# A gated cross-attention block with a routed feed-forward: keys staged first in each GpSimd slot, router weights cast in slot 2, and the first router step in two parts

## The chip, the cores and the metric

The kernel runs on one core of a Trainium2 chip. The metric is device time in microseconds (us), from the runtime's measurement of one execution. A core has five engines that run beside each other, each through its own queue in strict order: TensorE (PE) does matmuls and transposes into PSUM, VectorE (DVE) and ScalarE (ACT) read and write PSUM and SBUF, GpSimd (POOL) works on SBUF only, and SyncE (SP) issues DMAs. They meet at semaphores: an instruction that waits holds all that is queued behind it on its engine.

## What is computed

x is 16 batches of 128 tokens of 128 features; the context is 16 batches of 77 rows of 96.

```python
def xattn(x, y):                       # 16 heads of 8 features
    q = x @ Wq.T + bq;  k, v = split(y @ Wkv.T + bkv)
    att = softmax(q k / sqrt(8), over the 77 rows)
    return (att v) @ Wo.T + bo

def ffn(x):                            # 4 rounds, 4 experts, 2 of them per token
    cur = x
    for r in range(4):
        logits = cur @ Wg[r] + bg[r]
        vals, idx = top_k(logits, 2);  w = softmax(vals)
        cw = sum(one_hot(idx, 4) * w)
        y = gelu(cur @ W1[e] + b1[e]) @ W2[e] + b2[e]      # for each expert e
        cur = cur + sum_e(cw[e] * y[e])
    return cur

x = x + tanh(g0) * xattn(layernorm(x), ctx)
x = x + tanh(g1) * ffn(layernorm(x))
```

## The kernel before

All tensors stay on chip. There are two parts. The first is attention, in 16 **slots**, b = 0 to 15, one batch each, software-pipelined over the engines. The second is the experts: 16 steps (4 rounds of 4 chunks of 512 tokens) of 4 experts, 64 units, each unit an `up` and a `down` of TensorE, in three matmuls for each product (high by high, low by high, high by low parts), with gelu and the high parts on ScalarE and the low parts on VectorE.

What an engine does in a slot is written by hand, in the order of the code of its block, and tables (`K_AT`, `XN_AT`, `MOMENTS`, `SPLIT_X` and others) say which slot holds an extra step. In slot b:

- TensorE computes `scores(b + 1)` (line 1261), transposes the exponents' inputs of batch b in three groups (line 1275), projects the output of batch b - 2 (`project_o`, line 1310), and weighs the values of batch b - 1, called PV(b - 1) (lines 1297 and 1303). `scores(b)` waits for `k_st` of batch b, which is the keys spread over head-masked rows, and for the subtracted scores of batch b - 1. It does not wait for the exponentials. Slots 2, 5 and 8 hold transposes of the normalised x (line 1225), slots 10 and 13 transposes of the second normalisation's x (line 1321), slots 13 and 15 the logits of routers 0 and 1 (lines 1336 and 1337), slot 15 the transpose of router 0's weights (line 1383). Then `up(0)` starts, and PV(15) follows it.
- VectorE normalises the output of batch b - 2 (`normalise_o`: a reciprocal, line 918, writes `rT_sb`; line 922 writes `oT_sb`), takes the least score of batch b + 1 (line 902, in two halves), adds the residual of batch b - 3 (line 928) and subtracts (line 911). Behind these come the extra steps: moments of a layer norm (lines 862 and 865), the split of a chunk into high and low parts (`split_x`, lines 943 and 945), the router, the weights.
- ScalarE subtracts the other half of the scores (line 717), takes the exponentials in three groups (line 727) and moves some results out of PSUM. `gate` (line 743) is the tanh of a router step, `move_cwT` (line 762) moves the transposed weights. After the last slot come gate(1), a table load and the gelus.
- GpSimd stages the keys (`stage_k`, line 597, two batches ahead of the slot), ends the layer norms (`rstd_of`, lines 567 and 569; four normalisations at a time, lines 576 and 586), adds a bias to x (line 606), makes the low parts of the expert weights (`split_w`, lines 615 and 617) and the small tables of the router (`expert_order`, lines 554 to 560).
- SyncE loads inputs, places the values' pieces, and spreads the routed weights over the partitions.

**The first router step** is spread over slots 12 to 15. In slot 12 VectorE makes three copies of the router weights `wg_in` (line 1144 a cast into `wg_s`, line 1146 the rest of it, line 1149 `wg_w`). In slot 13 `router(0)` adds two logits parts and a bias (lines 1000 and 1002) and ranks the four experts (lines 1010 to 1028, nine small operations that end in `half_d`). ScalarE takes the tanh in slot 14, VectorE makes the weights in slot 14 (`weights(0)`, lines 1042 and 1050) and splits chunk 1. Slot 15 holds the moments of chunk 2 and `router(1)` with all its eleven operations. `stage_k` stands behind the other work of a slot from slot 2 on:

```python
                if b < 2:
                    stage_k(b + 2)
...
                if b - W_LAG in W_AT:
                    split_w(W_AT.index(b - W_LAG))
                if 2 <= b < B - 2:
                    stage_k(b + 2)
```

Of the kernel before, what the change touches and what calls it, by code (L numbers as in the profile page):

```python
# [15 lines left out]
def flamingo_gated_block(  # L16
# [59 lines left out]
    with ExitStack() as stack:  # L76
# [105 lines left out]
        gates_ld = sem("gates_ld")  # L182
        moe_ld = sem("moe_ld")
        out_st = sem("out_st")
        c_zero = sem("c_zero")
# [100 lines left out]
        CWT0_AT = 15  # L286
        GATE0_SLOT = 14
        ROUTER0_SLOT = 13
        WEIGHTS0_SLOT = 14
        ROUTER1_SLOT = 15  # L290
        K_AT = {8: 3}
# [113 lines left out]
        MOMENTS = {3: (0, 2), 5: (0, 3), 8: (1, 0), 10: (1, 1), 15: (1, 2)}  # L405
        SPLIT_X = {10: 0, 14: 1}

# [3 lines left out]
        def LG(q):  # L411
            return bank(("LG", q))[:, 0:TC * 2 * E]
# [31 lines left out]
        def _(sp):  # L444
# [15 lines left out]
            sp.dma_start(bg_row[:, :], bg.rearrange("r e -> (r e)").unsqueeze(0)  # L460
                          .to_broadcast([P, ROUNDS * E])).then_inc(moe_ld, 16)
            sp.dma_start(wg_in[:, :, :], Wg.rearrange("r h e -> h r e")).then_inc(moe_ld, 16)
            def place_v(c):
# [52 lines left out]
        def _(pool):  # L516
# [92 lines left out]
            def split_w(p):  # L609

                s = slice(p * WP, (p + 1) * WP)
                if p == 0:
                    pool.wait_ge(w_hi, 32)
                    pool.wait_ge(moe_ld, 16 * 4)
                nc.gpsimd.tensor_tensor(w1_lo[:, s], w1_in[:, s], w1_hi[:, s].bitcast(F32),
                                        ALU.subtract).then_inc(w_split, 1)
                nc.gpsimd.tensor_tensor(w2_lo[:, s], w2_in[:, s], w2_hi[:, s].bitcast(F32),
                                        ALU.subtract).then_inc(w_split, 1)
# [13 lines left out]
            for b in range(B):  # L632
                if b < 2:
                    stage_k(b + 2)
# [14 lines left out]
                if b - W_LAG in W_AT:  # L649
                    split_w(W_AT.index(b - W_LAG))  # L650
                if 2 <= b < B - 2:
                    stage_k(b + 2)
                if b % TC == 0:
# [14 lines left out]
        def _(act):  # L668
# [112 lines left out]
            for b in range(B):  # L781
                c, r = b // TC + 1, b % TC
                exponentials(b, 2)
                if b == GATE0_SLOT:
                    gate(0)
                if b not in BUSY and b + 1 < B:
                    subtract_most(b + 1)
                exponentials(b, 1)
                if b in XT_AT:
                    move_cur(XT_AT.index(b))  # L790
                if b == CWT0_AT:
                    move_cwT(0)
                if b in XN_AT:
                    move_xn(XN_AT[b])
                if b in BUSY and b + 1 < B:
                    subtract_most(b + 1)
                if b in Q_AT:
                    stage_q(Q_AT[b])
                exponentials(b, 0)
                if b in V_AT:  # L800
                    move_v(V_AT[b])
                if b in K_AT:
                    move_k(K_AT[b])
# [49 lines left out]
        def _(dve):  # L853
# [121 lines left out]

            def router(q):

                if q == 0:
                    dve.wait_ge(order_ready, 2)
                t = [gate_ops(q)]  # L980

# [10 lines left out]
                bgr = bg_row[:, r * E:(r + 1) * E].unsqueeze(1).to_broadcast([P, T, E])  # L992
                if q < 2:
                    written(dve, ("LG", q))
                    dve.wait_ge(moe_ld, 16 * 4)
                else:
                    dve.wait_ge(logits_done, q - 1)
                if q < 2:
                    lg_v = LG(q).rearrange("p (t n) -> p t n", t=T)
                    step(nc.vector.tensor_tensor(lga[:, ts, :], lg_v[:, :, 0:E], bgr, ALU.add))  # L1000
                    settle()
                    step(nc.vector.tensor_tensor(lg[:, ts, :], lg_v[:, :, E:2 * E], lga[:, ts, :], ALU.add))
                else:
                    lg_v = ps[:, 6 if q < NC else 7, 0:T * 32].rearrange("p (t w) -> p t w", t=T)
                    step(nc.vector.tensor_tensor(lg[:, ts, :], lg_v[:, :, 0:E], bgr, ALU.add))
                settle()
# [104 lines left out]
            for b in range(B):  # L1111
# [9 lines left out]
                if b + 1 < B:  # L1121
                    subtract(b + 1)
                if b == WEIGHTS0_SLOT:
                    weights(0)
                if b in MOMENTS:
                    moments(*MOMENTS[b])
                if b in NORMALISE:
                    normalise(NORMALISE[b])
                if b == 0:
# [5 lines left out]
                    copy_k(2)  # L1135
                if b == ROUTER0_SLOT:
                    router(0)
                if b in SPLIT_X:
                    split_x(SPLIT_X[b])
                if b == ROUTER1_SLOT:  # L1140
                    router(1)
                if b == 12:
                    dve.wait_ge(moe_ld, 16 * 4)
                    nc.vector.tensor_copy(wg_s[:, :, 0, :], wg_in[:, :, :]).then_inc(wg_split, 1)
# [419 lines left out]
```

## Time and profile before

| what | value |
|---|---|
| runs of the kernel before | 466.62 us median of 3 (466.54 to 467.97) |
| the profiled execution | 466.59 us |
| its span, first to last instruction | 464.9 us |
| granted TensorE clock, of full speed | 0.999 |
| TensorE busy | 451.3 us, 97% |
| VectorE busy | 366.3 us, 79% |
| ScalarE busy | 360.0 us, 77% |
| GpSimd busy | 70.0 us, 15% |

Attention fills the span to about 91 us, the experts the rest. The profile follows the work that ended last back from the end; 85% of the span on that chain is TensorE, 7% VectorE, 3% issue, 2% ScalarE. The rows of the next sections are from the trace of that execution. A row of a timeline has the start in us, the duration in us, the engine, the line of the kernel, the operation, what is written and read, the shapes and the count of merged instructions; a bracket at the end is the time for which the engine had been idle before, and what released it. "PE" is TensorE's matmul side.

### The profile page before, as it was taken

The numbers are of one execution on the slowest core, as the hardware profiler recorded it, in microseconds if no ns is written. First come the engines' busy times: TensorE is split into PE (matmuls) and PEld (weight loads), VectorE is DVE, ScalarE is ACT, GpSimd is POOL, SyncE is SP. The second block draws the span as 40 slices with busy tenths as digits, with TensorE's granted clock in tenths as the row PEclk, the third lists the DMA queues.
The fourth block names the chain that finished last, engine by engine and source line by source line (L and its number), as shares of the span: only waits on it lengthen the run. The fifth ranks groups of instructions, "written<-read, shape, count | busy, mean of one in ns | idle before, by whom it ended". The sixth has DMA issues, their size and how long they took to land.

```text
span 464.9 us, 8783 instructions
## 1 busy us (share of the span) xinstructions
PE 451.3 (97%) x2856; PEld 354.8 (76%) x2856; DVE 366.3 (79%) x729; ACT 360.0 (77%) x742; POOL 70.0 (15%) x109
## 2 busy tenths in 40 slices
PE   8988998899999999999999999999999999999996
PEld 6665766677877788878878887888788878888885
DVE  6987989988888779767876887688768876887776
ACT  5766877497878779877987798779877887787883
POOL 7928966125000000000000000000000000000000
PEclk9999999999999999999999999999999999999999
DMA  6690000050020200400030013002200310023001
GB/s 164 199 191 15 1 6 14 1 183 2 1 91 2 91 2 2 182 1 1 25 159 1 1 49 135 0 1 80 104 0 0 119 66 1 0 69 138 24 0 45
DMA packets 12892, 25.18 MB, mean 54 GB/s; under 512 B 4615, under 2 KB 8496, under 8 KB 10800
## 3 DMA queue, kind: packets, MB, share of 16 engines
q1 hardware_dynamic: 9408, 22.23, 13.7%
q0 software_dynamic: 2784, 2.18, 2.5%
q8 instruction: 23, 0.38, 0.3%
q10 hardware_dynamic: 656, 0.23, 0.2%
q14 instruction: 21, 0.17, 0.1%
HBM read 22.82 MB, written 1.18 MB: 52 GB/s over the span
## 4 chain that ended last, share of the span: by engine, by line
PE 85%; DVE 7%; issue 3%; ACT 2%; POOL 1%; DMA 1%; SPq 0%; DVEq 0%; POOLq 0%; ACTq 0%
PE ps L1408 13%; PE ps L1410 13%; PE ps L1409 13%; PE ps L1395 12%; PE ps L1397 12%; PE ps L1396 12%; PE ps L1275 2%; DVE least L902 2%; PE ps L1261 1%; PE ps L1297 1%; DVE rT_sb L918 1%; PE ps L1303 1%; DMA x_sb<-in_x_dram 1%; PE ps L1362 1%; DVE below L911 1%
## 5 line engine op out<-in xcount | busy, mean ns | idle before, releaser
L953 DVE TENSOR_TENSOR h_lo<-g_sb,h_hi 128x512 fp32r<-128x512 f32 x256 | 170.1, 688 | 76.3 <-ACT h_hi L818 76.3
L811 ACT ACTIVATE g_sb<-ps,cols 128x512 f32<-128x512 f32 x256 | 174.1, 691 | 41.4 <-PE ps L1397 40.8
L818 ACT ACTIVATE h_hi<-g_sb 128x512 fp32r<-128x512 f32 x256 | 155.5, 638 | 0.0
L1408 PE MATMUL ps<-h_hi,w_hi 128*128 128x512 f32 x252 | 102.4, 406 | 0.1
L1395 PE MATMUL ps<-x_hi,w_hi 128*128 128x512 f32 x256 | 101.0, 395 | 0.0
L1397 PE MATMUL ps<-x_hi,w_lo 128*128 128x512 f32 x256 | 100.1, 391 | 0.0
L1396 PE MATMUL ps<-x_lo,w_hi 128*128 128x512 f32 x256 | 99.7, 390 | 0.0
L1410 PE MATMUL ps<-h_hi,w_lo 128*128 128x512 f32 x252 | 99.6, 395 | 0.0
L1409 PE MATMUL ps<-h_lo,w_hi 128*128 128x512 f32 x252 | 99.4, 394 | 0.0
L1408 PEld LDWEIGHTS ps<-h_hi,w_hi 128*128 128x128 f32 x252 | 47.3, 188 | 14.0 <-issue 2.7
L1397 PEld LDWEIGHTS ps<-x_hi,w_lo 128*128 128x128 f32 x256 | 48.0, 188 | 11.4
L1396 PEld LDWEIGHTS ps<-x_lo,w_hi 128*128 128x128 f32 x256 | 48.1, 188 | 10.8
L1410 PEld LDWEIGHTS ps<-h_hi,w_lo 128*128 128x128 f32 x252 | 47.2, 187 | 11.7
L1395 PEld LDWEIGHTS ps<-x_hi,w_hi 128*128 128x128 f32 x256 | 48.0, 188 | 10.6
L1409 PEld LDWEIGHTS ps<-h_lo,w_hi 128*128 128x128 f32 x252 | 47.3, 188 | 9.9
L974 DVE TENSOR_TENSOR cur<-cur,contrib 128x512 f32<-128x512 f32 x63 | 43.2, 685 | 0.0
L727 ACT ACTIVATE probT<-ps 128x512 f32<-128x512 f32 (+1 forms) x48 | 25.0, 554 | 13.6 <-PE ps L1275 13.3
L717 ACT ACTIVATE below<-ps,least 128x77 f32<-128x77 f32 x128 | 29.3, 343 | 7.1 <-DVE least L902 7.0
L902 DVE TENSOR_REDUCE least<-ps 128x8 f32<-128x616 f32 x32 | 25.0, 791 | 2.1 <-PE ps L1261 1.9
L1275 PE MATMUL ps<-ident,below 128*128 128x128 f32 (+1 forms) x160 | 24.0, 280 | 0.6 <-ACT probT L727 0.5
L963 DVE SCALAR_TENSOR_TENSOR contrib<-ps,cols,cwb_even 128x512 f32<-128x512 f32 x32 | 23.9, 748 | 0.6 <-PE ps L1410 0.6
L963 DVE SCALAR_TENSOR_TENSOR contrib<-ps,cols,cwb_odd 128x512 f32<-128x512 f32 x31 | 23.1, 746 | 0.6 <-PE ps L1410 0.6
(126 smaller groups left out, 374.5 us busy)
## 6 DMA issues: line engine op xcount, KB each, us to landing
cwb_even<-cw_rows SPq DMA_DIRECT2D x8, 1024.0 KB, 5.4
cwb_odd<-cw_rows SPq DMA_DIRECT2D x8, 1024.0 KB, 5.0
w_hi<-in_L_ffn_W_dram POOLq DMA_DIRECT2D x2, 1024.0 KB, 10.8
w_in<-in_L_ffn_W_dram SPq DMA_DIRECT2D x1, 1024.0 KB, 5.5
x_sb<-in_x_dram SPq DMA_DIRECT2D x3, 256.0 KB, 5.4
out_dram<-xn SPq DMA_DIRECT2D x3, 256.0 KB, 2.5
ctxT<-in_ctx_dram SPq DMA_DIRECT2D x3, 115.5 KB, 5.2
v_st<-v_sb SPq DMA_DIRECT2D x14, 19.2 KB
```

Source lines behind the costliest of these rows:

```text
L811: nc.scalar.activation(g_sb[:, k, :], ps[:, k, :], ACT.Gelu_apprx_tanh, bias=b1_c[:, e * NF + k:e * NF + k + 1]).then_inc(gelu_done, 1)
L818: nc.scalar.activation(h_hi[:, u % 2, k, :], g_sb[:, k, :], ACT.Copy).then_inc(hi_done, 1)
L902: nc.vector.tensor_reduce(least[:, b % 2, :].rearrange("p (q h) -> p q h", q=NQ)[:, two, :], scores, AX.X, ALU.min).then_inc(least_done[ha ...
L953: nc.vector.tensor_tensor(h_lo[:, u % 2, k, :], g_sb[:, k, :], h_hi[:, u % 2, k, :].bitcast(F32), ALU.subtract).then_inc(lo_done, 1)
L963: nc.vector.scalar_tensor_tensor(out=contrib[:, u % 2, :], in0=ps[:, YB + u % 2, :], scalar=b2_c[:, e:e + 1], in1=cwb[i % NC][:, e, :], op ...
L974: nc.vector.tensor_tensor(cc, cc, contrib[:, u % 2, :], ALU.add).then_inc(added, 1)
L1395: mm(ps[:, k, :], w1_hi[:, w], x_hi[:, c, :], start=True, stop=False)
L1396: mm(ps[:, k, :], w1_hi[:, w], x_lo[:, c, :], start=False, stop=False)
L1397: mm(ps[:, k, :], w1_lo[:, w], x_hi[:, c, :], start=False, stop=True).then_inc(w1_done, 1)
L1408: mm(yb, w2_hi[:, w], hh, start=k == 0, stop=False)
L1409: mm(yb, w2_hi[:, w], hl, start=False, stop=False)
L1410: m = mm(yb, w2_lo[:, w], hh, start=False, stop=k == NF - 1)
```

## The change

`stage_k(b + 2)` becomes the first call of every GpSimd slot; it still waits for the scores of batch b. The three copies of the router weights go from slot 12 to slot 2; for them the loads of `bg_row` and `wg_in` get a semaphore of their own, `router_ld`, and the two expert weights keep `moe_ld`, now counted to two loads. `router(q)` takes its parts by name. The logits part of router 0 stays in slot 13, behind `split_x(1)`, which comes there from slot 14; the ranks part of router 0 goes to slot 15, ahead of the moments, and `weights(0)` goes to slot 15, between the moments and `router(1)`. ScalarE's `gate(0)` goes from slot 14 to slot 15, ahead of `move_cwT(0)` and so of the last group of exponentials. TensorE's and SyncE's order stay.

```diff
-        GATE0_SLOT = 14
-        ROUTER0_SLOT = 13
-        WEIGHTS0_SLOT = 14
-        ROUTER1_SLOT = 15
+        ROUTER_SLOT = 15
...
-        SPLIT_X = {10: 0, 14: 1}
+        SPLIT_X = {10: 0, 13: 1}
...
-                          .to_broadcast([P, ROUNDS * E])).then_inc(moe_ld, 16)
-            sp.dma_start(wg_in[:, :, :], Wg.rearrange("r h e -> h r e")).then_inc(moe_ld, 16)
+                          .to_broadcast([P, ROUNDS * E])).then_inc(router_ld, 16)
+            sp.dma_start(wg_in[:, :, :], Wg.rearrange("r h e -> h r e")).then_inc(router_ld, 16)
...
-                    pool.wait_ge(moe_ld, 16 * 4)
+                    pool.wait_ge(moe_ld, 16 * 2)
...
-                if b < 2:
+                if b + 2 < B:
                     stage_k(b + 2)
...
-                if 2 <= b < B - 2:
-                    stage_k(b + 2)
...
-                if b == GATE0_SLOT:
-                    gate(0)
...
                 if b == CWT0_AT:
+                    gate(0)
                     move_cwT(0)
...
-            def router(q):
-
-                if q == 0:
-                    dve.wait_ge(order_ready, 2)
-                t = [gate_ops(q)]
+            def router(q, parts=("logits", "ranks")):
+
+                t = [gate_ops(q) + (0 if "logits" in parts else 2)]
...
-                if q < 2:
-                    written(dve, ("LG", q))
-                    dve.wait_ge(moe_ld, 16 * 4)
...
+                if "logits" in parts:
+                    if q < 2:
+                        written(dve, ("LG", q))
+                        dve.wait_ge(router_ld, 16 * 2)
...
+                if "ranks" not in parts:
+                    return
+                if q == 0:
+                    dve.wait_ge(order_ready, 2)
                 settle()
...
-                if b == WEIGHTS0_SLOT:
-                    weights(0)
+                if b == ROUTER_SLOT:
+                    router(0, ("ranks",))
                 if b in MOMENTS:
                     moments(*MOMENTS[b])
+                if b == ROUTER_SLOT:
+                    weights(0)
...
-                if b == ROUTER0_SLOT:
-                    router(0)
                 if b in SPLIT_X:
                     split_x(SPLIT_X[b])
-                if b == ROUTER1_SLOT:
+                if b == LG_AT[0]:
+                    router(0, ("logits",))
+                if b == ROUTER_SLOT:
                     router(1)
-                if b == 12:
-                    dve.wait_ge(moe_ld, 16 * 4)
+                if b == 2:
+                    dve.wait_ge(router_ld, 16 * 2)
                     nc.vector.tensor_copy(wg_s[:, :, 0, :], wg_in[:, :, :]).then_inc(wg_split, 1)
```

The code is a few lines shorter, so a line number of the changed kernel is up to six lower than that of the same work before.

GpSimd, slots 2 to 5, before (the first row holds keys 4 and 5, the row behind the four normalisations key 6):

```order
L560 AFFINE_SELECT after<-after 128x16
L597 TENSOR_TENSOR k_st<-kT,head_mask 128x308 x2
L567 TENSOR_SCALAR veps<-mv 128x4
L569 TENSOR_TENSOR rstd<-veps,minus_half 128x4
L586 TENSOR_SCALAR xn<-x_sb,mv,rstd 128x128 x4
L597 TENSOR_TENSOR k_st<-kT,head_mask 128x308
L606 TENSOR_TENSOR x_sb<-x_sb,bo_row 128x512
```

The same place of the changed kernel:

```order
L558 AFFINE_SELECT after<-after 128x16
L595 TENSOR_TENSOR k_st<-kT,head_mask 128x308 x2
L565 TENSOR_SCALAR veps<-mv 128x4
L567 TENSOR_TENSOR rstd<-veps,minus_half 128x4
L584 TENSOR_SCALAR xn<-x_sb,mv,rstd 128x128 x4
L604 TENSOR_TENSOR x_sb<-x_sb,bo_row 128x512
L595 TENSOR_TENSOR k_st<-kT,head_mask 128x308
```

The pair now holds keys 5 and 6 (key 4 went ahead of the router tables), and the key behind the bias is key 7: key 6 went from behind the four normalisations to ahead of the statistics.

VectorE, end of slot 14 and start of slot 15, before:

```order
L911 TENSOR_TENSOR below<-least,ps 128x616
L1042 TENSOR_SCALAR wgt<-th 128x16
L1050 SCALAR_TENSOR_TENSOR cw<-rank,wgt 128x4x4
L943 CAST x_hi<-cur 128x512
L945 TENSOR_TENSOR x_lo<-cur,x_hi 128x512
L918 RECIPROCAL rT_sb<-ps 128x128
L922 TENSOR_TENSOR oT_sb<-ps,rT_sb 128x128
L928 SCALAR_TENSOR_TENSOR x_sb<-ps,tgates,x_sb 128x128
L862 BN_STATS stats<-x_sb 128x6 x4
L865 BN_AGGR mv<-stats 128x2 x4
L1000 TENSOR_TENSOR lga<-ps,bg_row 128x16
L1002 TENSOR_TENSOR lg<-ps,lga 128x16
```

VectorE, slot 15 of the changed kernel from its reciprocal on, as far as the ranks' last operation:

```order
L913 RECIPROCAL rT_sb<-ps 128x128
L917 TENSOR_TENSOR oT_sb<-ps,rT_sb 128x128
L923 SCALAR_TENSOR_TENSOR x_sb<-ps,tgates,x_sb 128x128
L1008 TENSOR_TENSOR beat_ge<-lg 128x64
L1009 TENSOR_TENSOR beat_gt<-lg 128x64
L1011 TENSOR_TENSOR beat_ge<-beat_ge,before 128x64
L1013 TENSOR_TENSOR beat_gt<-beat_gt,after 128x64
L1016 TENSOR_TENSOR beat_ge<-beat_ge,beat_gt 128x64
L1018 TENSOR_REDUCE rank<-beat_ge 128x16
L1021 SCALAR_TENSOR_TENSOR sel_lg<-rank,lg 128x16
L1024 TENSOR_REDUCE sel_sum<-sel_lg 128x4
L1026 SCALAR_TENSOR_TENSOR half_d<-sel_sum,lg 128x16
```

The ranks of router 0 now stand between the residual and the moments, and the weights and the split of chunk 1 are gone from in front of the reciprocal.

VectorE, slot 2 of the changed kernel:

```order
L897 TENSOR_REDUCE least<-ps 128x8 x2
L906 TENSOR_TENSOR below<-least,ps 128x616
L1144 CAST wg_s<-wg_in 128x4x4
L1146 TENSOR_TENSOR wg_s<-wg_in,wg_s 128x4x4
L1149 COPY wg_w<-wg_in 128x4x4
L913 RECIPROCAL rT_sb<-ps 128x128
```

The three copies of the router weights came there from the end of slot 12, ahead of the reciprocal of batch 1.

## Rows read from the trace of the kernel before

**Rows 1.** Stretches: length, busy PE, PEld, DVE, ACT, POOL (instructions), clock, DMA share, GB/s
```profile
94.00:103.00 9.00, 8.93 (x85) 7.00 (x84) 6.81 (x15) 8.77 (x17) 1.33 (x2) 1.00 0.56 198
103.00:420.00 317.00, 316.99 (x1426) 252.25 (x1425) 247.22 (x472) 256.71 (x471) 6.75 (x6) 1.00 0.12 46
```
**Rows 2.** TensorE's timeline, unit 0 of the experts
```profile
101.41 0.50 PE L1408 MATMUL ps<-h_hi,w_hi 128*128 128x512 f32 x1
```
**Rows 3.** VectorE's timeline, slots 14 and 15
```profile
82.87 0.95 DVE L918 RECIPROCAL rT_sb<-ps 128x128 f32<-128x128 f32 x1
...
86.56 0.17 DVE L1042 TENSOR_SCALAR wgt<-th 128x16 f32<-128x16 f32 x1
...
86.86 0.42 DVE L943 CAST x_hi<-cur 128x512 fp32r<-128x512 f32 x1
...
87.92 0.95 DVE L918 RECIPROCAL rT_sb<-ps 128x128 f32<-128x128 f32 x1
...
90.57 0.14 DVE L1000 TENSOR_TENSOR lga<-ps,bg_row 128x16 f32<-128x16 f32 x1
...
90.95 0.22 DVE L1010 TENSOR_TENSOR beat_ge<-lg 128x64 f32<-128x64 f32 x1
...
92.81 0.95 DVE L918 RECIPROCAL rT_sb<-ps 128x128 f32<-128x128 f32 x1
```
**Rows 4.** TensorE's timeline, scores(6) and scores(13)
```profile
36.69 0.80 PE L1261 MATMUL ps<-k_st,q_st 32*128 32x308 f32 x8 [1.62 <-POOL k_st L597]
...
71.50 0.80 PE L1261 MATMUL ps<-k_st,q_st 32*128 32x308 f32 x8 [1.04 <-ACT probT L727]
```
**Rows 5.** GpSimd's timeline, normalisations in slot 10, key 13
```profile
56.92 3.13 POOL L576 TENSOR_SCALAR xn<-x_sb,mv,rstd 128x128 f32<-128x128 f32 x4
...
70.70 0.70 POOL L597 TENSOR_TENSOR k_st<-kT,head_mask 128x308 f32<-128x308 f32 x1
```
**Rows 6.** VectorE's timeline, start of slot 6
```profile
42.36 0.96 DVE L918 RECIPROCAL rT_sb<-ps 128x128 f32<-128x128 f32 x1 [1.02 <-PE ps L1303]
```
**Rows 7.** TensorE's timeline, scores(10) in slot 9, transposes in slot 10
```profile
55.62 0.80 PE L1261 MATMUL ps<-k_st,q_st 32*128 32x308 f32 x8
...
62.10 0.66 PE L1321 MATMUL ps<-ident,xn 128*128 128x128 f32 x4
```
**Rows 8.** All engines' timeline, statistics and normalisations of chunk 2, weights(1)
```profile
90.75 0.23 POOL L567 TENSOR_SCALAR veps<-mv 128x4 f32<-128x4 f32 x1 [14.03 <-DVE mv L865]
...
92.20 3.13 POOL L576 TENSOR_SCALAR xn<-x_sb,mv,rstd 128x128 f32<-128x128 f32 x4
...
94.27 0.32 DVE L1042 TENSOR_SCALAR wgt<-th 128x16 f32<-128x16 f32 x1
```
**Rows 9.** VectorE's timeline, end of slot 12, start of slot 13
```profile
74.87 1.88 DVE L1144 CAST wg_s<-wg_in 128x16 fp32r<-128x16 f32 x1
...
76.95 0.95 DVE L918 RECIPROCAL rT_sb<-ps 128x128 f32<-128x128 f32 x1
```
**Rows 10.** TensorE's timeline, scores of slots 7, 8, 13, 14, oT(12)
```profile
46.42 0.80 PE L1261 MATMUL ps<-k_st,q_st 32*128 32x308 f32 x8
...
50.44 0.80 PE L1261 MATMUL ps<-k_st,q_st 32*128 32x308 f32 x8
...
75.23 0.80 PE L1261 MATMUL ps<-k_st,q_st 32*128 32x308 f32 x8
...
81.00 0.80 PE L1261 MATMUL ps<-k_st,q_st 32*128 32x308 f32 x8
...
84.20 0.49 PE L1310 MATMUL ps<-wo_t,oT_sb 128*128 128x128 f32 x2 [1.59 <-DVE oT_sb L922]
```
**Rows 11.** GpSimd's timeline, its last instruction before 90 us
```profile
76.00 0.72 POOL L597 TENSOR_TENSOR k_st<-kT,head_mask 128x308 f32<-128x308 f32 x1
```
**Rows 12.** VectorE's timeline, start of slot 3
```profile
26.25 0.96 DVE L918 RECIPROCAL rT_sb<-ps 128x128 f32<-128x128 f32 x1 [1.80 <-PE ps L1303]
```
**Rows 13.** SyncE's timeline, the load of the router weights
```profile
6.91 0.43 SPq L462 DMA_DIRECT2D wg_in<-in_L_ffn_Wg_dram  x1
```

More of the change, by code:

```diff
@@ L183, in flamingo_gated_block @@
         moe_ld = sem("moe_ld")
+        router_ld = sem("router_ld")
         out_st = sem("out_st")
@@ L992, in router @@
                 bgr = bg_row[:, r * E:(r + 1) * E].unsqueeze(1).to_broadcast([P, T, E])
-                if q < 2:
-                    written(dve, ("LG", q))
-                    dve.wait_ge(moe_ld, 16 * 4)
[L996 to L1005, printed above, removed]
+                if "logits" in parts:
+                    if q < 2:
+                        written(dve, ("LG", q))
+                        dve.wait_ge(router_ld, 16 * 2)
+                    else:
+                        dve.wait_ge(logits_done, q - 1)
+                    if q < 2:
+                        lg_v = LG(q).rearrange("p (t n) -> p t n", t=T)
+                        step(nc.vector.tensor_tensor(lga[:, ts, :], lg_v[:, :, 0:E], bgr, ALU.add))
+                        settle()
+                        step(nc.vector.tensor_tensor(lg[:, ts, :], lg_v[:, :, E:2 * E], lga[:, ts, :], ALU.add))
+                    else:
+                        lg_v = ps[:, 6 if q < NC else 7, 0:T * 32].rearrange("p (t w) -> p t w", t=T)
+                        step(nc.vector.tensor_tensor(lg[:, ts, :], lg_v[:, :, 0:E], bgr, ALU.add))
+                if "ranks" not in parts:
+                    return
+                if q == 0:
+                    dve.wait_ge(order_ready, 2)
                 settle()
```

## The prediction, made before the result was known

> **What bounds the kernel now.** I read the busy table of stretches first. From 103 us on TensorE is busy 316.99 of 317.00 us [rows 1]: the 64 expert steps are TensorE's own work, nothing that the change touches runs there, and what attention wins or loses ahead of them moves the end one for one, as long as they start in the same order. So only the start of that steady part matters. The stretch 94 to 103 belongs to ScalarE, busy 8.77 of 9.00 [rows 1]: after the gate of router 1 come the first gelus, the high parts, the copy of chunk 2. TensorE's last stop, at 101.41 [rows 2], is where it waited for the low parts behind that chain. So the start of the experts is set by the moment at which VectorE ends router(1), 92.81 (the reciprocal behind it starts there [rows 3]). I follow the attention slots to that moment. "rT(b)" is VectorE's reciprocal that opens the normalising of batch b; "key b" the staging of k_st for batch b on GpSimd; scores(b), PV(b) are TensorE's.
>
> **Keys first.** TensorE's timeline shows two slots in which scores start late: scores(6) at 36.69 after 1.62 idle, released by k_st, and scores(13) at 71.50 after 1.04 [rows 4]. The second is put down to probT, but key 13 runs 70.70 to 71.40 on GpSimd [rows 5] and scores do not wait for probT, so I take it for the key too. Each stands behind four normalisations of 3.13 us together [rows 5]. With the key ahead of them, each is ready microseconds early.
> Key 6: TensorE goes on 1.6 earlier. VectorE waited 1.02 for TensorE at 42.36 [rows 6], so it follows, and slots 6 to 11 move by the whole 1.6. Key 13: 1.0 more on TensorE. Sum there 2.6.
> What is late next is in slot 10: key 12 now stands ahead of the normalisation of chunk 0 and waits for scores(10), which start at 55.62 [rows 7]; shifted, they end near 54.8. Key 12 takes 0.7 [rows 5], the statistics 1.45 (as from 90.75 to 92.20 [rows 8]), and the run that was 56.92 to 60.05 [rows 5] ends near 60.2, about as before. TensorE wants it at 62.10 less 1.6, 60.5 [rows 7]. Covered, by 0.3 only; if that fails it costs a few tenths.
>
> **Router weights to slot 2.** In slot 12 the cast of 16 columns took 1.88 at 74.87 and rT(11) started at 76.95 [rows 9], 2.1 in all for three tiny instructions, while TensorE had already gone past PV(11) and begun scores(14) at 75.23 [rows 10]. The cast ended at 76.75, when GpSimd's last instruction (76.00 + 0.72) ended [rows 11], so I read it as blocked by GpSimd, not as its own price. Removed, rT(11) follows PV(11): 75.3 - 2.6 = 72.7 in place of 76.95, that is 4.2 earlier.
> In slot 2 VectorE then had 1.80 idle ahead of 26.25 [rows 12]. The three cost between 0.5 (three like the 0.17 of other 16-column work [rows 3]) and 2.1 (blocked again); GpSimd waits for statistics there, so I take the low end. Cost at most 0.3, forecast nothing. The new wait, for wg_in, stands in front of normalising batch 1, but that 8 KB transfer is issued at 6.91 [rows 13], 17 us ahead.
>
> **Slot 13.** The ranks leave it: 90.95 to 92.81, 1.86 of the like step [rows 3]; split_x(1) comes in, 86.86 to 87.92, 1.06 [rows 3]. VectorE's slot was 76.95 to 82.87, 5.92, and becomes 5.1. TensorE's slot, 75.23 to 81.00, 5.8 [rows 10], holds a transpose of x and the logits and now bounds it. So rT(12) is at 72.7 + 5.8 = 78.5, 4.4 earlier. Bank release: logits 0 are read by about 77.9, TensorE wants that bank at 79.3.
>
> **Slot 14.** VectorE took 82.87 to 87.92, 5.05 [rows 3], and TensorE stood 1.59 for its oT(12) at 84.20 [rows 10]. Out go weights(0), 86.56 to 86.86, 0.30, and split_x(1), 1.06 [rows 3], leaving 3.7. TensorE's plain slot is 46.42 to 50.44, 4.0 [rows 10], so rT(13) comes at 82.5: 5.4 earlier than 87.92. ScalarE loses gate(0) here, which only fills idle time.
>
> **Slot 15 gives back.** Ranks (1.86) and weights(0) (0.30) now stand ahead of router(1) on VectorE, with nothing beside them that covers them: 2.16. From rT(13) to the start of router(1) was 87.92 to 90.57, 2.65, and router(1) takes 90.57 to 92.81, 2.24 [rows 3]. Now 82.5 + 2.65 + 2.16 + 2.24 = 89.6 against 92.8: 3.2 earlier. The weights are made at 82.5 + 2.65 + 1.86 = 87.0 to 87.3; TensorE arrives at their transpose at about 87.3 (82.5 + one slot of 4.0 + the logits), and up(0) starts near 87.5, where it had started at 91.6. Exp of the last group comes behind gate(0) and cwT on ScalarE, near 88.1, long before PV(15) at 90.5. The moments end at 87.0, GpSimd's last-but-one normalisation near 91.7 and TensorE wants its transpose at 92.2: covered. So TensorE is about 4 early and ScalarE's chain behind router(1) 3.2 early; the chain is the later one and decides.
>
> **Sum.** -1.6 (key 6) -1.0 (key 13) -1.6 (cast; 4.2 in all up to there) -0.2 (slot 13) -1.0 (slot 14) +2.2 (slot 15) = -3.2. The profiled execution took 466.59 (span 464.9 and 1.7 around it), the median of runs is 466.62. Forecast 463.4.
> Bounds: key 13 in VectorE's time may be worth 0.5 less (probT was the releaser); cast in slot 2 +0.3; slot 10 +0.4; weights(1), made while GpSimd normalised, took 0.32 for its first instruction [rows 8] in place of 0.17, so weights(0) may cost 0.4 more if both of its instructions and the wait between them double. Not all at once: up to +1.0. Below, a slot 13 bounded by VectorE (5.1 for 5.8) would give -0.7. Own range 462.7 to 464.4.
>
> **Rivals.**
> A, the keys win nothing: another input holds slot 5 (the transposes of chunk 2 need the same run of normalisations, which ended where key 6 began, 36.69 less 0.1 and 0.7, at 35.9, against 36.7 wanted), or slot 10's cover fails in full, or the V pieces, which SP issues behind ScalarE's copy, hold slot 13. Then the 1.6 of key 6 is gone: 465.0. For it: covers under 1 us. Against: every one has a positive margin.
> B, no change: the upstream gain ends at about 2.2 instead of 5.4, for instance if both keys' 2.6 turn into other waits and TensorE's slots 13 and 14 do not shrink; then slot 15 eats it. About 466.4. Against: TensorE's 1.59 stop at 84.20 has no other cause than VectorE's work that leaves.
> C, slower: the collision moves instead of going away. weights(0) begins with a tensor_scalar from and to SBUF at 87.0, the moment when the moments end and GpSimd starts statistics and normalising, a run that went from 90.75 to 95.33 (92.20 + 3.13) [rows 8], ending 4.7 after the moments. If it is blocked to the end of that run, as the cast was to the end of three GpSimd instructions, it ends at 91.8, router(1) at 94.3 and not 92.8: +1.5 on 466.6, 468.1, slower. It decides from a block of 3.2 on. For it: the cast's 1.88. Against: the same tensor_scalar under the same kind of run took 0.32 at 94.27 [rows 8], and here it is issued at the same moment as GpSimd's first instruction or before it.
> The Trainium skill, "SBUF — State Buffer", Who interferes with whom, says that a cast or tensor_scalar on VectorE can use the port pair that GpSimd has, that the first comer holds it for its whole instruction and the other blocks fully. The slow cast agrees in kind, but it outlasted more than one GpSimd instruction, and the 0.32 is no full block; by the rule alone the wait would be one GpSimd instruction, 0.8 to 1.0, and the forecast 464.3.
> D, the change does not do what it says: the cast's 1.88 is its own price. It then leaves slot 12 anyway and costs 0.3 in slot 2: 463.7, within the range.
>
> **Chances.** Forecast (with D) 0.69, A 0.15, B 0.08, C 0.08. The 8 in 10 range takes in the forecast's own range and most of A: 462.5 to 465.2. About 0.3%, 1.4 us, is what a measurement of this kernel tells from no change. Faster by more: the forecast and about three quarters of A, 0.80. Within: the rest of A, B and a little of C, 0.13. Slower by more: 0.07.
>
> **What the profile after would show.** No wait for k_st ahead of scores(6) and scores(13); scores(6) near 35.1. The cast at about 24.5, of 0.2. rT(11) near 72.7, rT(12) 78.5, rT(13) 82.5; no stop of TensorE at oT(12). router(1) ending near 89.6, gate and table load right behind it, first gelu near 91.2, TensorE's last stop at 98.2. Wrong if the cast is still 1.9, if x of chunk 0 is waited for in slot 10, if weights(0) takes over 1 us, or if a new stop stands in slots 5 to 13.

## The result, and the profile after

| | before | changed |
|---|---|---|
| median of the runs | 466.74 us (4 runs, 466.54 to 467.97) | 463.5 us (4 runs, 463.26 to 463.65) |
| profiled execution | 466.59 us | 463.65 us |
| its span | 464.9 us | 461.9 us |
| TensorE busy | 451.3 us | 452.0 us |

The ratio is 0.993, with a 95% interval of 0.9919 to 0.9942: faster by 0.7%, 3.2 us. The forecast was 463.4. Rows below are of timelines unless said otherwise: start, duration, engine, line and operation, and in brackets the idle time ahead and its releaser.

The stretches of the changed kernel (length, busy PE, PEld, DVE, ACT, POOL, clock, DMA share, GB/s), 3 us earlier than those of [rows 1]:

```profile
91.00:100.00 9.00, 8.62 (x84) 6.78 (x83) 6.61 (x15) 8.77 (x17) 1.20 (x2) 1.00 0.62 203
100.00:417.00 317.00, 316.99 (x1426) 252.26 (x1425) 247.35 (x472) 256.71 (x471) 6.75 (x6) 1.00 0.12 46
```

The experts are the same work in the same time, to the hundredth. The start of them has moved. TensorE's rows, from scores(6), which had waited 1.62 for key 6 at 36.69 [rows 4], to the last stop, which was at 101.41 [rows 2]:

```profile
35.38 0.80 PE L1261 MATMUL ps<-k_st,q_st 32*128 32x308 f32 x8
...
69.27 0.80 PE L1261 MATMUL ps<-k_st,q_st 32*128 32x308 f32 x8
...
73.28 0.80 PE L1261 MATMUL ps<-k_st,q_st 32*128 32x308 f32 x8
...
80.27 0.49 PE L1310 MATMUL ps<-wo_t,oT_sb 128*128 128x128 f32 x2
...
83.39 1.13 PE L1275 MATMUL ps<-ident,below 128*128 128x128 f32 x6 [0.50 <-ACT probT L723]
...
88.10 0.28 PE L1383 MATMUL ps<-ident,cw 128*16 128x128 f32 x1 [0.50 <-DVE lg L996]
...
98.48 0.50 PE L1408 MATMUL ps<-h_hi,w_hi 128*128 128x512 f32 x1
```

scores(6) at 35.38 and scores(13) at 69.27 carry no bracket: neither key is waited for. oT(12) at 80.27 has lost its stop of 1.59 [rows 10]. The last stop ends at 98.48, 2.93 earlier.

VectorE from rT(10) to the end of router(1), with the ranks of router 0 from 84.40 and weights(0) at 87.40:

```profile
69.22 0.96 DVE L913 RECIPROCAL rT_sb<-ps 128x128 f32<-128x128 f32 x1 [0.22 <-PE ps L1303]
...
73.22 0.96 DVE L913 RECIPROCAL rT_sb<-ps 128x128 f32<-128x128 f32 x1 [0.22 <-PE ps L1303]
...
78.93 0.96 DVE L913 RECIPROCAL rT_sb<-ps 128x128 f32<-128x128 f32 x1 [0.56 <-PE ps L1303]
...
82.94 0.96 DVE L913 RECIPROCAL rT_sb<-ps 128x128 f32<-128x128 f32 x1 [0.23 <-PE ps L1303]
...
84.40 0.22 DVE L1008 TENSOR_TENSOR beat_ge<-lg 128x64 f32<-128x64 f32 x1
...
86.20 0.87 DVE L857 BATCH_NORM_STATS2 stats<-x_sb 128x6 f32<-128x128 f32 x4
...
87.40 0.14 DVE L1040 TENSOR_SCALAR wgt<-th 128x16 f32<-128x16 f32 x1
...
87.67 0.17 DVE L994 TENSOR_TENSOR lga<-ps,bg_row 128x16 f32<-128x16 f32 x1
...
89.89 0.95 DVE L913 RECIPROCAL rT_sb<-ps 128x128 f32<-128x128 f32 x1
```

rT(11), rT(12) and rT(13) now have a bracket: VectorE waits for TensorE, where before it waited for nothing ahead of them [rows 3, 9]. router(1) ends at 89.89 in place of 92.81 [rows 3], 2.92 earlier; the span is 3.0 shorter. The row at 89.89 is the reciprocal behind router(1), as the one at 92.81 was. On ScalarE the table load and the first gelus follow:

```profile
90.24 1.28 ACT L806 ACT_TABLE_LOAD   x1
91.53 1.27 ACT L806 ACTIVATE g_sb<-ps,cols 128x512 f32<-128x512 f32 x2
```

### The profile page after: what moved, and what is told of

The parts are those of the page before. It is cut to its first block, busy times and chain, and to the rows that moved or that the text cites. A ratio compares the mean times of both kernels' runs of the same rounds, so it can differ in the third digit from the quotient of the medians.

```text
span 461.9 us, 8784 instructions
## 1 busy us (share of the span) xinstructions
PE 452.0 (98%) x2856; PEld 355.4 (77%) x2856; DVE 364.3 (79%) x729; ACT 359.9 (78%) x742; POOL 70.0 (15%) x109
## 4 chain that ended last, share of the span: by engine, by line
PE 89%; DVE 6%; issue 2%; ACT 1%; DMA 1%; SPq 0%; POOL 0%; DVEq 0%; POOLq 0%
PE ps L1408 13%; PE ps L1410 13%; PE ps L1409 13%; PE ps L1395 12%; PE ps L1397 12%; PE ps L1396 12%; PE ps L1275 3%; PE ps L1297 2%; PE ps L1261 2%; PE ps L1303 2%; DVE least L897 1%; DVE rT_sb L913 1%; DMA x_sb<-in_x_dram 1%; PE ps L1310 1%; PE ps L1362 1%
## 5 line engine op out<-in xcount | busy, mean ns | idle before, releaser
L739 ACT ACTIVATE th<-half_d 128x32 f32<-128x32 f32 (+1 forms) x10 | 2.3, 225 | 27.6 <-DVE half_d L1026 27.6
```

## The experiments

**Theory**: the time is set by the moment at which router(1) ends; keys 6 and 13 and the GpSimd block of the cast are what the change takes from it, and the move of the ranks is worth what VectorE is behind by. **Rivals**: the keys win nothing (A), the cast's 1.88 is its own price (D), and the router's move is what gains.

### One part alone

`keys_only`: the kernel before with the keys first.

```diff
-                if b < 2:
+                if b + 2 < B:
                     stage_k(b + 2)
...
-                if 2 <= b < B - 2:
-                    stage_k(b + 2)
```

> Only the staging of the keys goes first in each GpSimd slot; router weights and router as before. Theory (the cast in slot 12 is blocked by GpSimd's run, and slots 13 to 15 are then bound by VectorE as before): scores(6) 1.6 early, scores(13) about 2.4 early, but the cast waits for the low parts of the weights that GpSimd now runs until about 74.7, so rT(11) comes near 75.0 in place of 76.95: about 464.7, -1.9. Rival (the cast's 1.88 is its own price): rT(11) near 74.6, 464.3, and the cast's duration stays 1.88. Rival A of the prediction (keys win nothing): 466.6.

`cast_only`: the three copies in slot 2, with `router_ld` as in the change.

```diff
-                if b == 12:
-                    dve.wait_ge(moe_ld, 16 * 4)
+                if b == 2:
+                    dve.wait_ge(router_ld, 16 * 2)
```

> Only the three copies of the router weights go to slot 2. Theory: cast about 0.2 in slot 2, hidden in VectorE's stop of 1.8; rT(11) follows PV(11) at 75.3 in place of 76.95, slots 13 to 15 keep their lengths on VectorE: 465.0, -1.6. Rival (the 1.88 is the cast's own price): the cast takes 1.88 in slot 2 too, and the time is 465.3. Rival (another wait takes its place in slot 13): no change.

`router_only`: the changed kernel with its keys and its copies put back.

```diff
-                if b + 2 < B:
+                if b < 2:
                     stage_k(b + 2)
...
                     split_w(W_AT.index(b - W_LAG))
+                if 2 <= b < B - 2:
+                    stage_k(b + 2)
...
-                if b == 2:
+                if b == 12:
                     dve.wait_ge(router_ld, 16 * 2)
```

> Only the router step is split and moved (split_x(1) to slot 13, ranks, weights(0) and gate(0) to slot 15); keys and cast as before. Theory (slot 15 gives back all that slots 13 and 14 gain, since VectorE's work from rT(11) on is the same and it never waits): rT(13) near 85.8 in place of 87.9, then 2.16 more: 466.6, no change. Rival (the move of the router is worth its 1.2 us by itself, since it takes TensorE's stop at oT(12) away): 465.4.

Measured against 466.92 us for the kernel before: keys alone 464.82 (0.9951, interval 0.9939 to 0.9963), cast alone 464.82 (0.9951, 0.9938 to 0.9964), router alone 466.77 (0.9996, 0.9988 to 1.0004). Rival A is out: the keys alone bring 2.1 us (2.4 by the spans, 464.9 and 462.5). The cast alone brings 2.1 (1.7 by the spans, 463.2). The medians can't place these two apart, since the runs of either lie within 0.9 of each other; the traces put the keys at 2.2 and the cast at 1.6 (the table below, rT(11) counted from rT(1)). The router's move alone brings nothing. In the trace of `keys_only`, VectorE and then GpSimd:

```profile
72.55 1.86 DVE L1142 CAST wg_s<-wg_in 128x16 fp32r<-128x16 f32 x1
...
74.61 0.95 DVE L916 RECIPROCAL rT_sb<-ps 128x128 f32<-128x128 f32 x1
```
```profile
72.30 0.70 POOL L597 TENSOR_TENSOR k_st<-kT,head_mask 128x308 f32<-128x308 f32 x1
72.96 0.72 POOL L615 TENSOR_TENSOR w_lo<-w_in,w_hi 128x256 fp32r<-128x256 f32 x1
73.65 0.72 POOL L617 TENSOR_TENSOR w_lo<-w_in,w_hi 128x256 fp32r<-128x256 f32 x1
```

The cast has moved earlier by 2.3 with everything around it and lasts 1.86 again. It ends at 74.41 and GpSimd at 74.37, as in [rows 9, 11]. In `cast_only` the same instruction at 24.80 takes 0.17: the 1.88 is not its own price (rival D is out). `keys_only` by itself does not tell the two apart: rT(11) came at 74.61, the rival's 74.6 and not the theory's 75.0. The theory had put the end of GpSimd's run at 74.7, and it was 74.37.

### Two parts

`keys_cast` has the diffs of `keys_only` and `cast_only`, and the router as before.

> Keys first and cast in slot 2, router as before. Theory (VectorE sets the time from rT(11) on, and moving the router only leaves it waiting for TensorE in slots 13 and 14): rT(11) near 73.2, then 5.92, 5.05 and 4.89 as before, router(1) ends near 89.1: 462.8, 0.7 below the changed kernel. Rival (the router's move is part of the gain): 464.5, 1 us above the changed kernel.

`cast_router` is the changed kernel with the keys behind again, `keys_router` the changed kernel with the copies in slot 12 again:

```diff
-                if b + 2 < B:
+                if b < 2:
                     stage_k(b + 2)
...
                     split_w(W_AT.index(b - W_LAG))
+                if 2 <= b < B - 2:
+                    stage_k(b + 2)
```

> The changed kernel without the keys (each key again behind the other work of its GpSimd slot): cast in slot 2 and the router split. Theory (slot 15 costs 2.16 whatever stands before; slots 13 and 14 give back only down to TensorE's 5.8 and 4.0): rT(13) near 85.1, router(1) ends near 92.1: 1.0 slower than the cast alone, 465.8. Rival (the router's move costs nothing, as with the router alone): 464.8.

```diff
-                if b == 2:
+                if b == 12:
                     dve.wait_ge(router_ld, 16 * 2)
```

> The changed kernel with the copies of the router weights back in slot 12: keys first and the router split. Theory: the cast ends with GpSimd's run near 74.4, rT(11) near 74.6, VectorE is then behind TensorE by about 1.7 and slots 13 and 14 shrink for it almost in full (rT(13) near 83.4): 464.6, the same as the keys alone. So the router's move costs nothing where VectorE is behind, and 0.8 to 1.0 where it is not. Rival (the router's move always costs about 0.85): 465.6.

`keys_cast` took 462.66 (462.49 to 462.74; 0.9906, 0.9893 to 0.9919), less than the changed kernel. `cast_router` took 465.42 (0.9967, 0.9955 to 0.998), `keys_router` 464.39 (0.9945, 0.9932 to 0.9957). All three came out on the side of their theory, within 0.4 us (expected: 462.8, 465.8 and 464.6), though `cast_router` is only 0.6 above `cast_only`, where 1.0 was expected. Read from VectorE's timelines, with the idle time in the brackets of rT(12) and rT(13) summed; rT(1) is VectorE's reciprocal at the start of slot 3:

| kernel | rT(1) starts | rT(11) starts | rT(1) to rT(11) | router(1) ends | rT(11) to that end | idle in it | span | span less end |
|---|---|---|---|---|---|---|---|---|
| before | 26.25 | 76.95 | 50.70 | 92.81 | 15.86 | 0 | 464.9 | 372.1 |
| `router_only` | 26.17 | 76.87 | 50.70 | 92.86 | 15.99 | 0.23 | 464.9 | 372.0 |
| `keys_only` | 26.08 | 74.61 | 48.53 | 90.47 | 15.86 | 0 | 462.5 | 372.0 |
| `keys_router` | 25.89 | 74.40 | 48.51 | 90.38 | 15.98 | 0.23 | 462.4 | 372.0 |
| `cast_only` | 26.19 | 75.29 | 49.10 | 91.15 | 15.86 | 0 | 463.2 | 372.0 |
| `cast_router` | 25.76 | 74.85 | 49.09 | 91.33 | 16.48 | 0.63 | 463.4 | 372.1 |
| `keys_cast` | 26.14 | 72.92 | 46.78 | 88.79 | 15.87 | 0 | 460.9 | 372.1 |
| changed | 26.46 | 73.22 | 46.76 | 89.89 | 16.67 | 0.79 | 461.9 | 372.0 |

Three things are in this table. The last column: in eight kernels the span ends 372.0 to 372.1 after router(1), so that moment sets the time. The middle: with the router as it was, VectorE needs 15.86 or 15.87 from rT(11) to that moment and never waits. Where the router is moved, it waits, and the stretch is longer by that or a tenth less (0.12 to 0.13 for an idle time of 0.23, 0.62 for 0.63, 0.81 for 0.79). The move takes next to no work off VectorE; it takes it out of slots 13 and 14, which TensorE then bounds, and puts it into slot 15, where nothing covers it. The third is the column from rT(1) to rT(11): it falls into four pairs, 50.70 with neither part, 48.51 and 48.53 with the keys, 49.09 and 49.10 with the cast, 46.76 and 46.78 with both, whatever the router does. rT(1) itself scatters by 0.7 us, and the edits don't explain it: in the trace of `cast_slot7` below, which up to there differs from the kernel before only in a semaphore of two loads, it is at 26.46. So two traces are compared by these stretches, and not by absolute times.

The rows of `keys_cast` for rT(11), rT(12), rT(13) and the end of router(1):

```profile
72.92 0.96 DVE L917 RECIPROCAL rT_sb<-ps 128x128 f32<-128x128 f32 x1 [0.23 <-PE ps L1302]
...
78.85 0.95 DVE L917 RECIPROCAL rT_sb<-ps 128x128 f32<-128x128 f32 x1
...
83.91 0.95 DVE L917 RECIPROCAL rT_sb<-ps 128x128 f32<-128x128 f32 x1
...
88.79 0.95 DVE L917 RECIPROCAL rT_sb<-ps 128x128 f32<-128x128 f32 x1
```

No bracket on the last three. Against the rows of the changed kernel rT(13) is 1 us later here and the end 1.1 earlier: the 2.1 that slot 15 saves. Of the 1.1, 0.3 is the earlier start of this trace, and 0.8 the shorter stretch. TensorE has one stop of half a microsecond in slot 14, and it costs nothing, since VectorE waits for nothing there:

```profile
83.31 1.13 PE L1274 MATMUL ps<-ident,below 128*128 128x128 f32 x6 [0.51 <-ACT probT L726]
...
97.39 0.50 PE L1407 MATMUL ps<-h_hi,w_hi 128*128 128x512 f32 x1
```

The last stop is at 97.39, 1.1 before that of the changed kernel. The medians say the same: the router's move costs 463.5 less 462.66, 0.8 us, with both other parts there (the runs of the two do not overlap, though the intervals of their ratios touch), 0.6 with the cast alone (465.42 and 464.82, runs that just overlap), and nothing that can be measured otherwise (464.39 and 464.82 with the keys alone, 466.77 and 466.92 with neither, runs that overlap in both).

### What blocked the cast

[rows 9, 11] and `keys_only` show the cast end together with GpSimd's last instruction. Two readings are possible: it waits for as long as GpSimd works on two-input operations back to back, or for a short fixed number of instructions. And is it the cast that is shut out, or any operation? `cast_slot7` puts the copies in slot 7, where GpSimd has seven such operations in a row ahead of it, `cast_slot9` in slot 9, beside the normalisations, which read one tensor and two columns of scalars.

```diff
-                if b == 12:
-                    dve.wait_ge(moe_ld, 16 * 4)
+                if b == 7:
+                    dve.wait_ge(router_ld, 16 * 2)
```

> The kernel before with the three router-weight copies at the end of slot 7, where GpSimd runs from 48 to 55 us without a stop (low parts, keys, a bias, all of them two-input operations). Theory 1 (the cast is blocked until GpSimd's run ends): the cast starts near 50.1 and lasts to about 55.2, some 5 us; TensorE loses about 4: 468.5. Theory 2 (it is blocked for one GpSimd instruction, as an exclusive port would have it): 0.2 to 0.9 us, covered by VectorE's stops in slots 8 and 9: 464.8. Theory 3 (1.9 us whenever GpSimd is busy, or its own price in a late slot): 1.9, about 465.8.

`cast_slot9` has 9 for the 7.

> The kernel before with the three copies at the end of slot 9. VectorE gets there near 59.4, while GpSimd is in its four normalisations (one SBUF input each) until 60.0, with two low parts and a key (two inputs each) close behind until 62.0. Theory (VectorE's cast can slip in between one-input operations of GpSimd, as weights(1) did with 0.32, and is shut out only by back-to-back two-input ones): 0.2 to 0.7 us, hidden in the stop of 1.05, about 464.8. Rival (any run of GpSimd shuts it out to its end, the 0.32 was luck): 2.6 us, and 466.3 or more.

`max_slot7` is `cast_slot7` with the copy written as an operation on two operands in SBUF, which gives the same values:

```diff
-                    nc.vector.tensor_copy(wg_s[:, :, 0, :], wg_in[:, :, :]).then_inc(wg_split, 1)
+                    nc.vector.tensor_tensor(wg_s[:, :, 0, :], wg_in[:, :, :], wg_in[:, :, :], ALU.max).then_inc(wg_split, 1)
```

> The kernel before with the three copies at the end of slot 7, the first of them written not as a copy but as the larger of wg_in and wg_in, an operation with two SBUF inputs and the same result. Theory (what waits is an operation that uses both of VectorE's SBUF reads, in whatever way): shut out as the cast was, 5.2 us, 470.7. Rival (only the one-input copy at double rate is shut out): 0.2 us, about 464.8.

`cast_slot7` took 470.71 (470.44 to 471.61; 1.0085, 1.0069 to 1.0101), slower than the kernel before. VectorE, then GpSimd from the cast's start to the end of the run, then TensorE:

```profile
50.27 5.24 DVE L1145 CAST wg_s<-wg_in 128x16 fp32r<-128x16 f32 x1
55.55 0.17 DVE L1147 TENSOR_TENSOR wg_s<-wg_in,wg_s 128x16 fp32r<-128x16 f32 x1
```
```profile
50.17 0.72 POOL L616 TENSOR_TENSOR w_lo<-w_in,w_hi 128x256 fp32r<-128x256 f32 x1
50.85 0.72 POOL L618 TENSOR_TENSOR w_lo<-w_in,w_hi 128x256 fp32r<-128x256 f32 x1
...
54.10 0.72 POOL L618 TENSOR_TENSOR w_lo<-w_in,w_hi 128x256 fp32r<-128x256 f32 x1
54.78 0.70 POOL L598 TENSOR_TENSOR k_st<-kT,head_mask 128x308 f32<-128x308 f32 x1
```
```profile
57.05 0.49 PE L1311 MATMUL ps<-wo_t,oT_sb 128*128 128x128 f32 x2 [4.12 <-DVE oT_sb L923]
```

The cast of 16 columns takes 5.24 us. It ends at 55.51, when the last of seven two-input operations of GpSimd ends, at 55.48 (the first had begun 0.1 before the cast). It isn't let in between any two of them. TensorE stands 4.12 for it. Against `cast_only` the time is 5.9 us longer, where theory 1 had 3.7 (468.5 less 464.8). What theory 1 left out is TensorE's clock. In 57.0 to 57.5 us, as the stop ends, it is still granted in full; from 57.5 to 60.5 the trace has it at 0.50 to 0.51, the lower of its two levels (1.2 of 2.4 GHz), and from 61.0 on at 1.00 again. The first part of PV in that stretch takes 1.52 for the 0.90 of other slots:

```profile
59.24 1.52 PE L1298 MATMUL ps<-probT,v_st 128*32 128x128 f32 x24
```

From oT at 57.05 to the next scores at 61.49 TensorE needs 4.44; in the kernel before it was 3.05 (52.57 to 55.62). So 4.1 is the stop, 1.4 the work at half clock, 0.3 the later start of this trace (rT(1) at 26.46 and 26.19). The stops of 1.62 and 1.59 in the kernel before had no such sequel: the clock is 1.00 from 33 to 37 and from 82 to 85 us.

`cast_slot9` (one run, 464.83 us beside 466.78 of the kernel before) and its neighbours on VectorE and GpSimd:

```profile
59.31 0.27 DVE L1145 CAST wg_s<-wg_in 128x16 fp32r<-128x16 f32 x1
59.61 0.17 DVE L1147 TENSOR_TENSOR wg_s<-wg_in,wg_s 128x16 fp32r<-128x16 f32 x1
```
```profile
56.77 3.13 POOL L577 TENSOR_SCALAR xn<-x_sb,mv,rstd 128x128 f32<-128x128 f32 x4
```

Inside the run of four one-input operations, which ends at 59.90, the cast takes 0.27, against 0.17 with an idle GpSimd. `max_slot7` (one run, 470.85 beside 466.78), VectorE and the end of GpSimd's run:

```profile
49.80 5.25 DVE L1145 TENSOR_TENSOR wg_s<-wg_in 128x16 fp32r<-128x16 f32 x1
```
```profile
54.32 0.70 POOL L598 TENSOR_TENSOR k_st<-kT,head_mask 128x308 f32<-128x308 f32 x1
```

5.25 us, to 55.05, with GpSimd at 55.02. So it isn't the cast as such, and not the number of its inputs.

Nor is it that GpSimd works without a gap. A timeline of less than a microsecond shows the four normalisations one by one. They start at 56.77, 57.56, 58.34 and 59.11, each is 0.80 long, and the next starts before that is over, just as in the two-input run (0.72 long, 0.68 apart). The cast, from 59.31 to 59.58, lies wholly inside the last of them:

```profile
59.11 0.80 POOL L577 TENSOR_SCALAR xn<-x_sb,mv,rstd 128x128 f32<-128x128 f32 x1
```

What GpSimd runs decides, then, but not alone. In the kernel before, VectorE's statistics of x, which read one tensor in SBUF, run inside the same stretch of two-input GpSimd work in which `cast_slot7` was held, and take the 0.86 that they take beside an idle GpSimd at 89.37:

```profile
54.08 0.86 DVE L862 BATCH_NORM_STATS2 stats<-x_sb 128x6 f32<-128x128 f32 x4
```

And a comparison with two inputs in SBUF takes its usual 0.22 to 0.23 beside a two-input GpSimd operation on 4 columns. GpSimd, then VectorE, in the changed kernel:

```profile
87.94 1.04 POOL L567 TENSOR_TENSOR rstd<-veps,minus_half 128x4 f32<-128x4 f32 x1
```
```profile
88.47 0.23 DVE L1011 TENSOR_TENSOR beat_ge<-beat_ge,before 128x64 f32<-128x64 f32 x1
```

Held were a cast and an operation on two operands, both in SBUF, beside two-input GpSimd work on 256 to 512 columns. Whether the form of GpSimd's instruction or its width makes the difference, and what sets the statistics apart, no run here separates.

### A faster version

`tuned` is `keys_cast` with the low parts of unit 0 ahead of the split of chunk 2, and with slot 14 added to those in which ScalarE subtracts its part of the next scores behind the second group of exponentials and not ahead of it.

```diff
-        BUSY = set(XN_AT) | set(Q_AT) | set(XT_AT) | set(LG_AT)
+        BUSY = set(XN_AT) | set(Q_AT) | set(XT_AT) | set(LG_AT) | {14}
...
             low(0, 1)
-            split_x(NC - 2)
             low(0, 2)
             low(0, 3)
+            split_x(NC - 2)
```

> Keys first and cast in slot 2, router as before, and two more moves: VectorE makes all four low parts of unit 0 before it splits chunk 2 (TensorE's stop of 0.24 at 97.4 goes), and ScalarE in slot 14 takes the second group of exponentials before it subtracts the scores (TensorE's stop of 0.51 at 83.3 goes in part; the subtraction comes 0.5 later and may itself be waited for). Theory: TensorE has no other stop from 67 us on, so 0.2 to 0.6 less than 462.7: about 462.3. Rival: the later subtraction takes the place of the exponentials, only 0.2: 462.5.

It took 462.2 us (461.89 to 462.8; 0.9903, 0.9887 to 0.992), which beats both kernels. Against `keys_cast` the ratios can't be told apart. By the trace only the first edit gains: the span, 460.2, ends 371.8 after router(1) and not 372.1, with no stop of TensorE left at 97.4. The second gains nothing. TensorE's stop of 0.51 for the exponentials gives way to one of 0.18 for VectorE's split, but from rT(11) to the end of router(1) it is 15.86, as in `keys_cast` (15.87). router(1) ends at 88.40, 0.4 earlier, because the trace starts earlier (rT(1) at 25.79, in `keys_cast` at 26.14).

## Why the prediction was right, step by step

| step | forecast | measured |
|---|---|---|
| scores(6) | 35.1, no wait | 35.38, no wait |
| rT(11) | 72.7 | 73.22 |
| rT(12) | 78.5 | 78.93 |
| rT(13) | 82.5 | 82.94 |
| router(1) ends | 89.6 | 89.89 |
| up(0) starts | 87.5 | 88.31 |
| first gelu | 91.2 | 91.53 |
| last stop of TensorE | 98.2 | 98.48 |
| the copy in slot 2 | 0.2 | 0.17 |
| time | 463.4 | 463.5 |

**What bounds it.** The steady part did not change, and the end of router(1) decides, which the last column of the table of eight kernels shows more plainly than the profile of before could.

**Keys and cast.** Both are real; together they are 4.26 by the medians (466.92 less 462.66) and 4.0 by the spans. Up to rT(11) the sum said 4.2 and the changed kernel shows 3.73 (76.95 to 73.22): this is the term that was mis-sized. 0.21 of the gap is the later start of this trace (rT(1) at 26.46, before at 26.25 [rows 12]). The copies in slot 2 are not its cause: `keys_cast` has them and is at 26.14. Counted from rT(1) the gain is 3.94.

Of that, the keys were put at 2.6 and are 2.16, by scores(14), from 75.23 [rows 10] to 73.28, less the 0.21. The missing 0.4 to 0.5 is in three places. Key 6 brings 1.52 of its 1.62 (36.69 to 35.38, plus 0.21), and key 13 0.92 of its 1.04 (71.50 to 69.27 is 2.44 with the 0.21, less the 1.52): about 0.1 us of each stop stays. And the slot behind key 13 is 0.28 longer: from a late scores(13) TensorE reached the next scores in 3.73 (71.50 to 75.23 [rows 4, 10]), from a punctual one in 4.01 (69.27 to 73.28), so a part of the 1.04 had been made up already. The cast is 1.8 (3.94 less 2.16) where 1.6 was said.

**Slot 10's cover.** GpSimd's normalisation of chunk 0 ran from 57.44 to 60.57, and TensorE took it without a wait:

```profile
57.44 3.13 POOL L574 TENSOR_SCALAR xn<-x_sb,mv,rstd 128x128 f32<-128x128 f32 x4
```
```profile
60.80 0.66 PE L1321 MATMUL ps<-ident,xn 128*128 128x128 f32 x4
```

0.2 of cover where 0.3 was forecast: a run of GpSimd that ends a quarter of a microsecond later would begin to take the key's gain away, which is the condition of rival A.

**Slots 13 to 15.** The sum said -0.2 -1.0 +2.2, a loss of 1.0. Measured against [rows 3, 9]: slot 13 is 5.71 (73.22 to 78.93) for 5.92, slot 14 is 4.01 (78.93 to 82.94) for 5.05, and rT(13) to the end of router(1) 6.95 (82.94 to 89.89) for 4.89: -0.2 -1.0 +2.1, a loss of 0.8. With 3.73 that makes the 2.92 of the end of router(1). That the time came within 0.1 of the forecast is in part luck: up to rT(11) the sum was 0.5 too good, 0.2 of it by the start of one trace, and slots 13 to 15 cost 0.2 less than it said. What the prediction did not say is what its own signs mean: that the router's move, on top of the other two parts, makes the kernel slower than leaving it out.

**The rivals.** A fell with `keys_only`, D with `cast_only`. B needed an upstream gain of 2.2 at rT(13): it was 4.98. C, a blocked weights(0), did not come: the rows of the changed kernel have it at 87.40 with 0.14 and its second operation done by 87.76, while GpSimd started the statistics at 87.58:

```profile
87.58 0.28 POOL L565 TENSOR_SCALAR veps<-mv 128x4 f32<-128x4 f32 x1 [12.83 <-DVE mv L860]
```

The bound of +0.4 for it was not needed either. **Not foreseen**: the transpose of the weights waited 0.50 at 88.10 for the second logits sum of router(1) (the bracket names `lg`), which now comes behind the weights; that is 0.5 of the 0.8 by which up(0) is later than forecast, and the other 0.3 is TensorE's arrival at 87.6 and not at 87.3. It costs nothing, since ScalarE's first gelu follows the table load, at 91.53, and the end of router(1) sets that.

## What to carry to other kernels

Find the moment from which the rest of the program takes a constant time, and measure each edit by that moment: here one row of VectorE predicted the span of eight kernels within 0.1 us. Moving work from a slot to a later one is free only while the engine that does it is behind; once the slots it leaves are bounded by another engine, the move costs the idle time that appears in brackets, so cost each part of a change on top of the others and not only the whole. A small cast or a small operation on two SBUF operands, beside a run of wide two-input GpSimd work, can cost as much as the rest of that run, so put it where GpSimd waits or does one-input work. If TensorE stands for it, look at the clock behind the stop too: here a stop of 4.12 us cost 1.4 more.

Before you read a gain of a few tenths from two traces, compare them at a moment ahead of the edit: here that moment alone differed by up to 0.7 us.

## What was not expected of the hardware

A VectorE operation of 16 columns, 0.17 us by itself, was held for 1.86 to 1.88 us by the end of a GpSimd run in slot 12, and for 5.24 us by seven two-input operations (0.70 to 1.26 each) in slot 7, for a cast as for a maximum of two operands in SBUF; beside one-input GpSimd work it took 0.27. VectorE's statistics, with one operand in SBUF, were not held beside the same two-input work (0.86 at 54.08). The Trainium skill, "SBUF — State Buffer", Who interferes with whom, has the first comer hold the port pair for its whole instruction. The kind of the block agrees; by that rule the wait would be at most one GpSimd instruction, and here it was all that stood back to back, while inside a one-input instruction of GpSimd there was no full block (0.27 for 0.17). Other work with two SBUF inputs ran freely where GpSimd was idle: the comparisons of the ranks took 0.22 each from 84.40 on, as before.
